# Gated delta rule and feed-forward on one core: where the two grams stand, where v is turned, and when the down parts begin

## What is computed

```
xn = layernorm(x)
# attention: 16 heads, keys of 16, values of 32
q, k, v = silu(causal_conv4(xn @ w))          # per channel, 4 taps
beta = 2*sigmoid(xn @ b_w.T + bias);  g = -exp(A_log)*softplus(xn @ a_w.T + dt_bias)
per token:  S = S*exp(g);  delta = (v - k@S)*beta;  S = S + outer(k, delta);  o = q@S
attn = (o * rsqrt(mean(o*o)) * silu(g_out)) @ o_w.T
# feed-forward: 4-bit weights with scales per group of 128
h = silu(xn @ Wg.T) * (xn @ Wu.T)             # 1408 wide
y = h @ Wd.T;  ffn = y / sqrt(mean(y*y) + 1e-6)
out = x + attn + ffn
```

## Time and profile before

| what | value |
|---|---|
| median of three runs | 3327.87 us |
| span of the profiled execution | 3330.7 us |
| TensorE matmuls busy | 3142.1 us, 94% |
| VectorE busy | 2390.6 us, 72% |
| GpSimd busy | 1918.8 us, 58% |
| ScalarE busy | 1667.4 us, 50% |
| chain that ended last, TensorE's share | 77% |
| chain that ended last, VectorE's share | 12% |

### The profile page before, as it was taken

The page is one execution under the profiler, slowest core; times in us unless marked ns, Lnnn a source line. Parts: engine busy times, 40 slices in busy tenths (PEclk is TensorE's granted clock), DMA queues, the critical chain, the costliest instruction groups (busy, mean ns, idle before and its releaser), DMA issues.

```text
span 3330.7 us, 118645 instructions
## 1 busy us (share of the span) xinstructions
PE 3142.1 (94%) x45632; PEld 2252.9 (68%) x45632; DVE 2390.6 (72%) x5408; ACT 1667.4 (50%) x3306; POOL 1918.8 (58%) x2865
## 2 busy tenths in 40 slices
PE   5999999999999999999999999999999999999995
PEld 4666766766666766666767767667667666767663
DVE  7677776777776777777777767777767777767772
ACT  3544554544554545554445545445545455544452
POOL 4566555666555665556665556665556655556652
PEclk8999999999999999999999999999999999999996
DMA  3111111111111111111111111111111111111111
GB/s 112 39 46 27 37 43 33 46 45 28 34 43 36 46 37 27 43 37 42 46 27 37 43 33 46 46 27 37 43 33 46 40 28 39 42 37 46 34 25 30
DMA packets 318318, 132.08 MB, mean 40 GB/s; under 512 B 277089, under 2 KB 278881, under 8 KB 317793
## 3 DMA queue, kind: packets, MB, share of 16 engines
q1 hardware_dynamic: 313824, 119.26, 14.3%
q10 hardware_dynamic: 4096, 6.42, 0.5%
HBM read 75.30 MB, written 50.33 MB: 38 GB/s over the span
## 4 chain that ended last, share of the span: by engine, by line
PE 77%; DVE 12%; issue 6%; POOL 2%; ACT 1%; ACTq 1%; DMA 1%; DVEq 0%; SPq 0%; POOLq 0%
PE PS L1166 17%; PE PS L1122 13%; PE PS L1153 8%; PE PS L1235 7%; PE PS L1154 7%; PE PS L1376 6%; DVE arena L893 4%; PE PS L1221 3%; PE PS L1300 2%; PE PS L1253 2%; DVE arena L378 2%; PE PS L1271 2%; PE PS L1391 2%; DVE arena L988 1%; PE PS L1178 1%
## 5 line engine op out<-in xcount | busy, mean ns | idle before, releaser
L893 DVE SCALAR_TENSOR_TENSOR arena<-PS,sc,arena 128x256 f32<-128x256 f32 x2112 | 1001.0, 482 | 253.0 <-ACT arena L613 152.2
L1153 PE MATMUL PS<-xh,wgu 128*128 128x256 f32 x2816 | 871.6, 341 | 35.9 <-DVE arena L893 35.4
L613 ACT ACTIVATE arena<-PS,sc 128x256 f32<-128x256 f32 x704 | 330.0, 474 | 759.0 <-PE PS L1154 700.3
L1154 PE MATMUL PS<-xl,wgu 128*128 128x256 f32 x2816 | 698.8, 282 | 0.0
L1166 PE MATMUL PS<-wdn,inner 128*128 128x512 f32 x1408 | 650.7, 592 | 0.0
L1153 PEld LDWEIGHTS PS<-xh,wgu 128*128 128x128 f32 x2816 | 531.2, 189 | 155.8 <-issue 84.2
L511 POOL TENSOR_TENSOR work<-arena 128x31 f32<-128x31 f32 (+15 forms) x992 | 511.9, 516 | 137.5 <-DMA arena<-scr_a 62.3
L515 POOL TENSOR_TENSOR arena<-arena,work 128x31 f32<-128x31 f32 (+15 forms) x992 | 542.1, 546 | 77.7
L1154 PEld LDWEIGHTS PS<-xl,wgu 128*128 128x128 f32 x2816 | 530.4, 188 | 83.2 <-issue 83.2
L1122 PE MATMUL PS<-xnT,wqkv 128*128 128x256 f32 x2048 | 485.6, 388 | 25.2 <-ACT inner L593 15.4
L1122 PEld LDWEIGHTS PS<-xnT,wqkv 128*128 128x128 f32 x2048 | 383.6, 192 | 93.1 <-ACT inner L593 16.4
(11 more groups left out here) (147 smaller groups left out, 4619.2 us busy)
## 6 DMA issues: line engine op xcount, KB each, us to landing
xt<-in_x SPq DMA_DIRECT2D x64, 256.0 KB, 2.8
scr_a<-arena SPq DMA_DIRECT2D x64, 256.0 KB, 2.4
arena<-scr_a SPq DMA_DIRECT2D x256, 64.0 KB, 3.2
obuf<-in_x SPq DMA_DIRECT2D x64, 256.0 KB, 2.8
scr_t<-arena SPq DMA_DIRECT2D x32, 512.0 KB, 2.7
arena<-scr_t SPq DMA_DIRECT2D x256, 64.0 KB, 2.3
out<-obuf SPq DMA_DIRECT2D x64, 256.0 KB, 2.0
wqkv<-in_wqkv ACTq DMA_DIRECT2D x1, 2048.0 KB, 14.3
```

The costliest lines, as they stand in the source:

```text
L613: eng.activation(fa[:, u % 4, :], PS[:, bank(u, 0), 0:NB * P], ACT.Copy, scale=sc[:, u % 2, KB * m:KB * m + 1]).then_inc(fa_scaled.sem, 1)
L893: eng.scalar_tensor_tensor(out=fa[:, u % 4, :], in0=PS[:, bank(u, k // 2), k % 2 * NB * P:][:, 0:NB * P], scalar=sc[:, u % 2, KB * m + k:K ...
L1153: eng.matmul(o, w, xh[:, k, :], start=True, stop=False)
L1154: ins = eng.matmul(o, w, xl[:, k, :], start=False, stop=True)
```

## The change

Both grams get columns of their own in banks 0 to 3 (0 to 255 for b = 0, 256 to 511 for b = 1), so `gram(1)` no longer waits for the products of `gram(0)`. TensorE's order becomes unit 2, unit 3, gram(0), gram(1), unit 4, unit 5, down(0), turns of v, unit 6 and on. `gram_products(0)` waits for both grams, and stands behind the two sums of squares of o on VectorE. v is turned in banks 6 and 7, which `turn_o` now has to wait for. Every down part stands two units earlier than before. The last two convolutions of v are done one by one (`conv_one`) behind `sums_of_squares(1)` and behind `products(1)`, the latter followed by the copy of the halo; the activation of v and its table load stand earlier on ScalarE. The layer norm is applied in two halves behind `hidden(7)` and `hidden(9)`.

```
@@ -753,10 +753,14 @@
             decay(0)
             u_rows(1)
             decay(1)
+            eng.preload_act_table_set(SILU)
             u_rows(2)
             masked_keys(0)
             u_rows(3)
             other_keys()
+            if n:
+                eng.wait_ge(*taps_done.at(n, NQKV))
+                eng.activation(qkv[:, 4:NQKV, :], qkv[:, 4:NQKV, :], ACT.Silu).then_inc(silu_done.sem, 1)
             gate_copy(0)
             gate_copy(1)
             masked_keys(1)
@@ -774,12 +778,9 @@
                 for b in range(NB):
                     eng.wait_ge(*o_copied.at(t, b + 1))
                     eng.activation(osq[:, b, :], sq[:, b, :], ACT.Square).then_inc(osq_done.sem, 1)
-            unit(3)
-            eng.preload_act_table_set(SILU)
             if n:
                 gate(0)
-                eng.wait_ge(*taps_done.at(n, NQKV))
-                eng.activation(qkv[:, 4:NQKV, :], qkv[:, 4:NQKV, :], ACT.Silu).then_inc(silu_done.sem, 1)
+                unit(3)
                 unit(4)
                 gate(1)
                 unit(5)
@@ -793,7 +794,7 @@
                 return
             for b in range(NB):
                 eng.wait_ge(*v_turned.at(n, b + 1))
-                eng.activation(R[:, b, :, 0:DV], PS[:, b, :].rearrange("p (h v) -> p h v", h=H),
+                eng.activation(R[:, b, :, 0:DV], PS[:, 6 + b, :].rearrange("p (h v) -> p h v", h=H),
                                ACT.Copy).then_inc(v_copied.sem, 1)
 
 
@@ -843,11 +844,10 @@
             eng.bn_aggr(mv[:, 0, :], st[:, 0, :]).then_inc(mean_part.sem, 1)
             eng.bn_aggr(mv[:, 1, :], st[:, 1, :]).then_inc(mean_done.sem, 1)
 
-        def layer_norm_apply(eng, m):
+        def layer_norm_apply(eng, m, b):
             eng.wait_ge(*rst_done.at(m, 2))
-            for b in range(NB):
-                eng.tensor_scalar(xt[:, b, :], xt[:, b, :], mv[:, b, 0:1], rst[:, b:b + 1], ALU.subtract,
-                                  ALU.mult).then_inc(xn_done.sem, 1)
+            eng.tensor_scalar(xt[:, b, :], xt[:, b, :], mv[:, b, 0:1], rst[:, b:b + 1], ALU.subtract,
+                              ALU.mult).then_inc(xn_done.sem, 1)
 
         def decode(eng, i):
 
@@ -863,6 +863,20 @@
                                      op0=ALU.bitwise_and, op1=ALU.bitwise_or).then_inc(f8_done.sem, 1)
 
         def dve_step(eng, t, n, more):
+            def conv_one(m):
+
+                if not n:
+                    return
+                for k in range(1, TAPS):
+                    if k == 1:
+                        eng.wait_ge(*tap0_done.at(n, m + 1))
+                    else:
+                        eng.wait_ge(*taps_part.at(n, 2 * m + k - 1))
+                    acc = qkv[:, m, :].rearrange("p (b t) -> p b t", b=NB)
+                    eng.scalar_tensor_tensor(out=acc, in0=cin[:, m, :, k:k + P], scalar=cw[:, m, k:k + 1], in1=acc,
+                                             op0=ALU.mult, op1=ALU.add).then_inc(
+                        (taps_done if k == TAPS - 1 else taps_part).sem, 1)
+
             def conv(m):
 
                 if not n:
@@ -975,14 +989,14 @@
             def gram_products(b):
                 if not n:
                     return
-                eng.wait_ge(*gram_out.at(n, b + 1))
+                eng.wait_ge(*gram_out.at(n, NB))
                 eng.wait_ge(*decay_done.at(n, b + 1))
 
                 def heads(ap):
                     return ap.rearrange("p (f g e i) -> p g f (e i)", f=NHALF, g=4, e=2)
 
-                Gq = PS[:, 0:4, 0:4 * CH].rearrange("p g (f n) -> p g f n", f=NHALF)
-                Gk = PS[:, 0:4, 4 * CH:8 * CH].rearrange("p g (f n) -> p g f n", f=NHALF)
+                Gq = PS[:, 0:4, 8 * CH * b:8 * CH * b + 4 * CH].rearrange("p g (f n) -> p g f n", f=NHALF)
+                Gk = PS[:, 0:4, 8 * CH * b + 4 * CH:8 * CH * (b + 1)].rearrange("p g (f n) -> p g f n", f=NHALF)
                 Eb = E[:, b, :, :].rearrange("p h i -> p (h i)")
                 eng.tensor_tensor(heads(kbq[:, b, :]), Gk, heads(Eb), ALU.mult).then_inc(a_done.sem, 1)
                 eng.tensor_tensor(heads(D[:, b, :, :].rearrange("p h i -> p (h i)")), Gq, heads(Eb),
@@ -1021,6 +1035,7 @@
             conv(4)
             keep_rows(1)
             sums_of_squares(1)
+            conv_one(6)
 
 
             state(0)
@@ -1028,29 +1043,27 @@
             products(0)
             state(1)
             products(1)
+            conv_one(7)
+            if n:
+                eng.tensor_copy(halo[:, :, :, :], cin[:, :, :, P:]).then_inc(halo_out.sem, 1)
             state(2)
             if n and more:
                 layer_norm_stats(eng, n.next())
             state(3)
-            if n and more:
-                layer_norm_apply(eng, n.next())
-            conv(6)
-            if n:
-                eng.tensor_copy(halo[:, :, :, :], cin[:, :, :, P:]).then_inc(halo_out.sem, 1)
 
 
             unit(0)
             unit(1)
             unit(2)
-            gram_products(0)
             if t:
                 for b in range(NB):
                     eng.wait_ge(*osq_done.at(t, b + 1))
                     eng.tensor_reduce(so[:, b, :], osq[:, b, :].rearrange("p (h v) -> p h v", v=DV), AX.X,
                                       ALU.add).then_inc(so_done.sem, 1)
+            gram_products(0)
             gram_products(1)
+            hidden(0)
             unit(3)
-            hidden(0)
             hidden(1)
             if not n:
                 result(0)
@@ -1064,6 +1077,8 @@
                 hidden(m)
                 if t and m in (6, 8):
                     result((m - 6) // 2)
+                if more and m in (7, 9):
+                    layer_norm_apply(eng, n.next(), (m - 7) // 2)
             eng.wait_ge(*res_loaded.at(n, 16 * NB))
             for i, b in enumerate((1, 0)):
                 if i == 0:
@@ -1079,7 +1094,8 @@
             eng.memset(S[:, :, :, :, :], 0.0).then_inc(zeroed.sem, 1)
             first = Tile(0, 0, first=True)
             layer_norm_stats(eng, first)
-            layer_norm_apply(eng, first)
+            for b in range(NB):
+                layer_norm_apply(eng, first, b)
             eng.wait_ge(first_loaded.sem, 16 * 2)
             eng.wait_ge(gup_loaded.sem, 32)
             for i in range(2):
@@ -1161,7 +1177,7 @@
             def down(m):
                 for b in (1, 0):
                     if m == 0:
-                        eng.wait_ge(*v_copied.at(n, NB))
+                        eng.wait_ge(*p_done.at(n, NB))
                     eng.wait_ge(*h_done.at(n, m + 1))
                     ins = eng.matmul(PS[:, b, :], inner[:, m, b * P:(b + 1) * P], wdn[:, m, :], start=(m == 0),
                                      stop=(m == FM - 1))
@@ -1341,16 +1357,15 @@
                     return
                 hold(eng, *knq_copied.at(n, 2 * (b + 1)))
                 hold(eng, *kb_copied.at(n, 1))
-                if b:
-                    hold(eng, *p_done.at(n, b))
-                elif t:
+                if b == 0 and t:
                     hold(eng, *o_copied.at(t, NB))
                 for f in range(NHALF):
                     for c in range(NC):
                         s = slice(c * CH, (c + 1) * CH)
                         for q in range(4):
                             r = slice(q * 32, (q + 1) * 32)
-                            o = PS[s, q, 0:8 * CH].rearrange("p (w n i) -> p n w i", w=2, i=CH)[:, 2 * f:2 * f + 2, :, :]
+                            o = PS[s, q, 8 * CH * b:8 * CH * (b + 1)].rearrange("p (w n i) -> p n w i", w=2,
+                                                                                 i=CH)[:, 2 * f:2 * f + 2, :, :]
                             ins = eng.matmul(o, kbT[r, b, f, s], knq[b][r, f, :, :, s], start=True, stop=True,
                                              skip_group_check=True)
                 ins.then_inc(gram_out.sem, 1)
@@ -1361,7 +1376,7 @@
                 for b in range(NB):
                     eng.wait_ge(*o_scaled.at(t, b + 1))
                     if n and b == 0:
-                        eng.wait_ge(*fa_done.at(n, 4))
+                        eng.wait_ge(*v_copied.at(n, NB))
                     for m in range(KB):
                         ins = eng.transpose(PS[:, 6 + b, m * P:(m + 1) * P], sq[:, b, m * P:(m + 1) * P], ident[:, :])
                     ins.then_inc(o_turned.sem, 1)
@@ -1462,25 +1477,22 @@
                 return
 
 
+            unit(5)
+            down(0)
             for b in range(NB):
                 eng.wait_ge(*silu_done.at(n, NC + 1))
-                eng.wait_ge(*p_done.at(n, NB))
+                eng.wait_ge(*fa_done.at(n, 4))
                 for m in range(4):
-                    ins = eng.transpose(PS[:, b, m * P:(m + 1) * P], qkv[:, 4 + m, b * P:(b + 1) * P], ident[:, :])
+                    ins = eng.transpose(PS[:, 6 + b, m * P:(m + 1) * P], qkv[:, 4 + m, b * P:(b + 1) * P], ident[:, :])
                 ins.then_inc(v_turned.sem, 1)
-            unit(5)
```

(10 more changed lines are left out.)

30 lines of the change are left out of this document (14 added, 16 removed).

## The result

The changed kernel takes 3360.41 us (median of four runs, 3359.6 to 3366.51), the kernel before in the same comparison 3328.64 us (3323.96 to 3334.64): ratio 1.0099, 95% interval 1.0087 to 1.0111. It is 31.8 us slower; forecast were about 20, with a range up to 3368. The profiled execution spans 3357.8 us, 27.1 more than before.

The account below looks back on a forecast made before the run. TensorE bounds the kernel before, but after the change the loop gram, solve, `t_times_r` does: 1.32 + 0.26 - 0.97 = 0.61 us per cycle, 31 cycles 18.9, plus 1.32 in the first tile: 20.2, giving 3348 us, range 3322 to 3368.

Parts of the forecast that it names:

- The bound and the second loop: TensorE bounds the kernel before; the tile-crossing loop gram, solve, `t_times_r` is only 1% of a tile behind.
- TensorE's own path: TensorE's work per tile, with gaps around grams and units 6 and 7 closed: 1.3 us shorter; 3288 us if kept, chance 0.14.
- A: End of the first gram product on VectorE, from which SyncE's transfers lead to the solve on GpSimd.
- A is later: First gram product waits for both grams and the sums of squares: 1.32 us later per tile, bounds 1.1 and 1.6.
- B: Start of `t_times_r(0)` on TensorE, which needs the solve's result read back.
- more solve for the layer norm: Layer norm halves on VectorE beside the solve hinder GpSimd: 0.26 us per tile, bounds 0 and 2 x 0.50.
- the rival in which GpSimd stands still for the halves: Each layer norm half holds GpSimd for its whole length: solve grows by 1.0 us, 3371 us, chance 0.10.
- The sum: Loop per tile: 1.32 later product plus 0.26 longer solve minus 0.97 spare, 0.61 us longer over 31 cycles.
- the forecast's 1.32 for the first tile: The first tile's own first gram product comes 1.32 us later, added once to the 31 cycles' 18.9 us.
- the spare time: How far the loop through the solve lies behind TensorE, ahead of `t_times_r(0)`: 0.97 us, mean of 1.20 and 0.75.
- The free edits: Split convolution of v, earlier activation and table load, moved turns of v and layer norm halves: cost nothing or tenths.

Follow-up runs that it names:

- the kernel before with the delay: Kernel before the change, with GpSimd's two memsets that prepare the solve moved behind its wait for the gram products: 3362.34 us, ratio 1.0108.
- the writes first: Changed kernel with both SyncE writes of the gram products issued ahead of the reads: 3288.7 us, ratio 0.9889 to the kernel before.
- the grams moved back: Changed kernel with both grams ahead of unit 3 on TensorE instead of behind it: 3359.27 us, ratio 1.0106 to the kernel before.
- the changed one with the delay: Changed kernel with GpSimd's two memsets that prepare the solve moved behind its wait for the gram products: 3412.5 us.

## Why the prediction was right

**The bound and the second loop.** Right. The loop gram, solve, `t_times_r` was 0.8 to 0.9 us a tile behind TensorE (2.94 to 2.15 in the changed kernel, 2.94 to 2.07 in the kernel before with the delay), forecast 0.97 from two tiles and the last step's 2.03. It carries the whole result: with it shortened the sign turns (3288.7), with a delay it grows.

**TensorE's own path.** Forecast 1.3 us per tile shorter, 3288 us if kept. With the writes first: 3288.7; 100.93 - 99.58 = 1.35. But the text was wrong on who brings it. It books the 1.3 us under the grams' new columns and says that the order of the down parts adds nothing more, though its own sum has down(0) behind unit 5. With the down parts at their old places the new columns bring nothing (3328.13). The down parts early without the new columns were not run, so it is shown that the saving needs them, not that they would bring it alone.

**A is later.** Forecast 1.32 us counted from B; measured 42.28 - 40.69 = 1.59. It falls in two. From unit 2 to the first product 3.13 became 4.29, 1.16. This is the mechanism as forecast: the last gram is out 0.19 us before the product starts, the sums end as it starts, and taking away the grams' hold alone brought nothing. The other 0.43 lie between B and unit 2 (36.88 to 37.31), which I had left as it was. 0.31 of them are idle time behind `t_times_r(0)` that the profile puts down to "issue" (0.86 us in the timeline above; in the mean 0.10 before, 0.41 now). Over all runs, kernels whose `t_times_r(0)` waits in most tiles have 36.95 to 37.40 from B to unit 2, the others 36.55 to 36.97. The cause stays open, and the term isn't firm: the execution of 3344.49 us with the grams moved back has the changed kernel's instructions up to unit 2 and 36.95 there. The 0.36 between the two is 11 us over the tiles, most of what lies between that execution and the other three.

**GpSimd.** Forecast 0.26 per tile more solve for the layer norm, bounds 0 and 1.0; measured 0.12, from 37.71 to 37.83, of which 0.08 go when the layer norm goes back. That is little above the scatter: the kernel before with the delay has 37.82 without any layer norm beside the solve. The Trainium skill, "SBUF — State Buffer", "Who interferes with whom", has the second of two such instructions wait for the whole of the first; here VectorE's half grows by 0.35 us, about the length of one of the solve's operations and not of the solve, and GpSimd's solve by 0.1 or less for both halves. So the rival in which GpSimd stands still for the halves (+1.0) didn't come.

**The sum.** 1.59 + 0.12 + 0.03 - 0.79 = 0.95 (0.94 by the tiles themselves) per tile, where 0.61 was forecast; 31 x 0.94 = 29.1. The first tile's A was to come 1.32 later and came 2.0 sooner (81.50 instead of 83.52), and 29.1 - 2.0 = 27.1 is the difference of the spans. This 2.0 is not the change's doing; it goes with the clock of the opening. Over the first 80 us the mean granted clock is 0.91 in five of the fourteen profiled executions, the changed kernel's among them, and their first A comes at 80.38 to 81.50. It is 0.87 to 0.89 in the other nine, the kernel before's among them, with A at 82.65 to 84.01. Both groups hold kernels of both orders, and within a group the orders differ by less than 1 us. So the forecast's 1.32 for the first tile did not show; why is open. The mis-sized terms are B to unit 2 (+0.43 against 0) and the spare time (0.79 against 0.97), and they outweigh the two that were put too high (unit 2 to the product, 1.16 against 1.32, and the solve, 0.12 against 0.26). That the total still lay well inside the range owes something to luck, since a term of 0.43 that the forecast lacked was partly made up by these two.

**The free edits** were free: 3325.91 with them alone.

**What stays open:** why executions of the changed kernel with one edit undone fall into two groups some 15 us apart (3342 and 3357 with the layer norm back, 3344 and 3360 with the grams moved), beyond the stretch from B to unit 2 in which most of the difference lies; and whether the layer norm costs the loop-bound kernel more than the 0.1 us of its solve.

## What to carry to other kernels

Look for loops that cross iterations before trusting busy shares: take each transfer or slow engine's chain from one tile to the next, add it up, and compare it with the tile's length; here 0.9 us of 101 stood between a gain of 40 us and a loss of 32. When an edit lets one engine run ahead by delaying the point at which a long chain starts, price the start of that chain first, and every queue by which it is entered. A wait that stands between two independent transfers on one queue (write, wait, read, write, wait, read) costs little until that chain binds; taking it out (write, write, wait, read, wait, read) was worth 5 us where TensorE bound and 72 us where the loop did. And when an edit has made a chain shorter, read how much it now has to spare before shortening it further: here it was 0.2 us, and two later edits lost more than that at the second entry.

## What was not expected of the hardware

Where the reads of the solve's result land just before `t_times_r(0)`, TensorE tends to lose time once more within the next small matmuls, for no release that the profile shows: 0.29 to 0.52 us per tile in the mean in the ten kernels in which B follows the last read's issue by 2.05 to 2.40 us, and 0.01 to 0.10 in the four in which it follows by 2.77 or more. A wait just before isn't needed for it: in the kernel with the writes first the 21 tiles without one have 0.28. And the layer norm beside GpSimd's many short operations took 0.85 us instead of 0.50 while the solve as a whole grew by 0.1. Last, the granted clock went to half for some 3.4 us in single steady tiles of some kernels (none in the kernel before, 4 in the changed one, 13 with the down parts back, 16 in the changed one with the delay), in all but ten cases 7 to 9 us after the start of unit 2, and behind the wait ahead of unit 5. A tile with such a fall took 0.2 to 0.5 us more in the kernels with the writes first.
